# Two blocks of nodes per transpose and per product in three node products of a four-layer graph network

## The reference, cut to what matters

```python
# layer 0: scatter of gated node rows
xp = x @ W_node.T + b_node
msg = gate[:, None] * xp[col]
summed = segment_sum(msg, row)
...
# layer 3: two convolutions
def gcn_conv(x, src, dst, W, b, n_nodes):
    ...
    h = x @ W
    msg = h[src] * norm[:, None]
    out = segment_sum(msg, dst)
    return out + b
h = relu(gcn_conv(x, src, dst, W1, b1, n))
return gcn_conv(h, src, dst, W2, b2, n)
```

## Time and profile before

| | us |
|---|---|
| median of 3 runs | 14080.94 |
| the runs | 14061.56, 14080.94, 14081.86 |
| the profiled execution | 14056.44 |
| its span, first to last instruction | 14053.5 |
| PE busy | 6581.5 (47%) |
| DVE busy | 6540.1 (47%) |
| ACT busy | 1956.0 (14%) |
| POOL busy | 8844.8 (63%) |

### The profile page before, as it was taken

One profiled execution on the slowest core, in us unless ns is written; L12 is line 12 of the kernel. 1 busy time (PEld: TensorE's weight loads), 2 busy tenths in 40 slices (PEclk: granted clock), 3 DMA queues, 4 the chain that ended last, 5 costly groups with the idle time before them and its releaser, 6 DMA issues.

```text
span 14053.5 us, 162350 instructions
## 1 busy us (share of the span) xinstructions
PE 6581.5 (47%) x40047; PEld 5632.1 (40%) x40048; DVE 6540.1 (47%) x13266; ACT 1956.0 (14%) x3268; POOL 8844.8 (63%) x8158
## 2 busy tenths in 40 slices
PE   5777777774555555788500000284333334333334
PEld 4777777774555555677400000173111112111112
DVE  5444444444666666899500000397434344434344
ACT  1111111111222222566300000000000001000000
POOL 2888888884777777100377777402777773777773
PEclk7666666666777777899655555697555555555555
DMA  4333333333444444333122222232111111111111
GB/s 96 18 18 18 18 18 18 18 18 62 126 126 127 126 126 127 107 98 99 50 54 54 54 54 55 61 97 63 39 39 39 39 39 33 39 39 39 39 39 26
DMA packets 851569, 827.49 MB, mean 59 GB/s; under 512 B 630205, under 2 KB 636579, under 8 KB 848948
## 3 DMA queue, kind: packets, MB, share of 16 engines
q0 software_dynamic: 450064, 387.16, 18.7%
q1 hardware_dynamic: 398252, 436.72, 9.9%
q10 hardware_dynamic: 3218, 3.20, 0.1%
HBM read 571.32 MB, written 255.06 MB: 59 GB/s over the span
## 4 chain that ended last, share of the span: by engine, by line
POOL 51%; issue 22%; PE 11%; DMA 8%; DVE 5%; SPq 1%; DVEq 1%; POOLq 0%; ACT 0%; ACTq 0%
POOL tab L728 21%; POOL aux L702 10%; POOL lane_tab L685 10%; DMA lane_tab<-rows,idx 7%; POOL buf_b L702 6%; POOL acc_w L702 4%; PE ps L1089 3%; PE ps L1200 1%; PE ps L979 1%; PE ps L1136 1%; PE ps L1122 1%; DVE buf_b L1658 1%; SPq L552 1%; POOL t_first_tab L713 1%; PE ps L963 1%
## 5 line engine op out<-in xcount | busy, mean ns | idle before, releaser
L728 POOL DMA_INDIRECT tab<-gcn_tab,idx x3136 | 2984.0, 952 | 1826.1 <-issue 1825.2
L685 POOL DMA_INDIRECT lane_tab<-rows,idx x1664 | 2597.7, 1561 | 661.8 <-issue 659.0
L1101 PE MATMUL ps<-ident_b,zero_b 128*128 128x512 bf16 x1664 | 773.2, 619 | 2917.7 <-issue 1551.2
L1737 DVE TENSOR_REDUCE buf_d<-ps 128x512 f32<-128x1536 f32 x416 | 731.1, 1757 | 2299.8 <-PE ps L1105 2299.8
L702 POOL DMA_INDIRECT aux<-att_tab,idx x1568 | 1486.9, 948 | 477.7 <-issue 477.7
L1101 PEld LDWEIGHTS ps<-ident_b,zero_b 128*128 128x128 bf16 x1664 | 182.0, 128 | 3282.1 <-issue 1788.3
L702 POOL DMA_INDIRECT buf_b<-src_tab,idx x832 | 838.3, 1008 | 414.1 <-issue 253.4
L1003 PE MATMUL ps<-ident,srcg 128*128 128x128 f32 x3328 | 695.2, 393 | 727.1 <-DVE srcg L1356 727.1
L702 POOL DMA_INDIRECT acc_w<-src_tab,idx x832 | 815.6, 980 | 253.6 <-issue 247.2
L1003 PEld LDWEIGHTS ps<-ident,srcg 128*128 128x128 f32 x3328 | 643.8, 297 | 772.7 <-DVE srcg L1356 772.5
L1179 PE MATMUL ps<-ident,acc_w 128*128 128x128 f32 x13 | 3.0, 422 | 1954.5 <-ACT idx L819 1954.5
(11 more groups left out here) (297 smaller groups left out, 14373.0 us busy)
## 6 DMA issues: line engine op xcount, KB each, us to landing
y_stash<-buf_c SPq DMA_DIRECT2D x208, 512.0 KB, 2.8
tab<-y_stash SPq DMA_DIRECT2D x208, 512.0 KB, 3.3
aux<-in_edge_attr_dram SPq DMA_DIRECT2D x1696, 32.0 KB
h_stash<-aux SPq DMA_DIRECT2D x196, 264.0 KB, 2.0
tab<-gcn_tab,idx POOLq DMA_INDIRECT x3136
buf_c<-h_stash SPq DMA_DIRECT2D x156, 264.0 KB, 2.7
lane_tab<-rows,idx POOLq DMA_INDIRECT x1664, 3.2
aux<-att_tab,idx POOLq DMA_INDIRECT x1568
```

Source lines behind the costliest of these rows:

```text
L685: pool.indirect_dma_start(lane_tab[k][:, :], bass.IndirectOffsetOnAxis(ap=idx[:, b, u:u + 1], axis=0), rows[:, b, u, 0:D1], None, compute_ ...
L728: pool.indirect_dma_start(g_rows[k][:, u, :], None, table[:, :], bass.IndirectOffsetOnAxis(ap=idx[:, k % RING, u:u + 1], axis=0)).then_inc ...
L1101: pe.matmul(ps[:, 4 * (q % 2) + c, :].rearrange("p (k f) -> p k f", f=P), zero_b[:, :], bc(ident_b[:, :].unsqueeze(1), [P, 4, P]), start=T ...
L1737: dve.tensor_reduce(g_sum[b], parts(4 * b), AX.X, ALU.add).then_inc(s.split_joined, 1)
```

## The change

The products of the first scatter and of both convolutions take two blocks at a time. A pair of blocks, 128 nodes x 128 features, is transposed at once, straight from `x_n` or `tab_d` without ACT's copy to `xs`. The weight stands twice on the diagonal of a 128x128 tile with zeros elsewhere (`twice_n` in the accumulator's space, `twice_g` in `aux`), so one product with 128 rows of contraction gives both blocks' results side by side. DVE makes the tile by a memset and two copies: once before the first product, and at the start of each `gcn`. The second copy of `w1` and `w2` in partitions 64 to 127 comes from two more DMAs. There are 7 steps (PAIRS) of 7 pairs, written out without a loop; DVE takes a step out of PSUM with one instruction. PE waits for ACT's kept source rows before the first product's transposes. The products of layers 1 and 2 keep their code.

```diff
+WPP = 2 * WPC
+PAIRS = W // WPP
+NODE_AT = (0, PAIRS, PAIRS + CHUNKS, PAIRS + 2 * CHUNKS, 2 * PAIRS + 2 * CHUNKS)
...
+        x_pairs = [aux_flat[:, xt_at + k * WPC * P:xt_at + (k + 1) * WPC * P] for k in range(2)]
+        twice_n, twice_g = acc_flat[:, 0:P], aux_flat[:, 2 * S:2 * S + P]
...
-        w12 = sb("w12", [D, 2, D])
+        w12 = sb("w12", [P, 2, D])
...
-            sp.dma_start(w12[:, 0, :], w1).then_inc(s.weights_loaded, 16)
-            sp.dma_start(w12[:, 1, :], w2).then_inc(s.weights_loaded, 16)
+            for at in (0, D):
+                sp.dma_start(w12[at:at + D, 0, :], w1).then_inc(s.weights_loaded, 16)
+                sp.dma_start(w12[at:at + D, 1, :], w2).then_inc(s.weights_loaded, 16)
...
+            def pair_copies(base):
+                for c in range(PAIRS):
+                    act.wait_ge(s.node_xt, c + (base + 1))
+                    act.wait_ge(s.node_products, c + (base + 1))
+                    act.activation(x_pairs[c % 2], ps_flat[:, (c % 2) * 1024:(c % 2) * 1024 + WPC * P], ACT.Copy).then_inc(s.node_xt_copied, 1)
...
-            node_copies(0, x_n)
+            pair_copies(NODE_AT[0])
...
+            def pair_product(base, view, rhs):
+
+                def transposes(c):
+                    at = (c % 2) * 1024
+                    for k in range(WPC):
+                        w = c * WPP + 2 * k
+                        last = pe.transpose(ps_flat[:, at + k * P:at + k * P + P], view[:, w:w + 2, :].rearrange("p w f -> p (w f)"), ident[:, :])
+                    last.then_inc(s.node_xt, 1)
+
+                transposes(0)
+                for c in range(PAIRS):
+                    if c + 1 < PAIRS:
+                        transposes(c + 1)
+                    pe.wait_ge(s.node_xt_copied, c + (base + 1))
+                    pe.wait_ge(s.node_evacuated, c + (base + 1))
+                    at = 2048 + (c % 2) * 1024
+                    for k in range(WPC):
+                        last = pe.matmul(ps_flat[:, at + k * P:at + k * P + P], x_pairs[c % 2][:, k * P:k * P + P], rhs, start=True, stop=True)
+                    last.then_inc(s.node_products, 1)
...
-            node_product(0, wt[0:D, TN:TN + D], D, 4)
+            pe.wait_ge(s.src_kept, 1)
+            pair_product(NODE_AT[0], x_n, twice_n)
...
-            node_product(3 * CHUNKS, w12[:, 0, :], D, 4)
+            pair_product(NODE_AT[3], tab_d, twice_g)
...
+            def twice(to, weight):
+                link(dve.memset(to, 0.0))
+                for at in (0, D):
+                    link(dve.tensor_copy(to[at:at + D, at:at + D], weight[at:at + D, :]))
+
+            twice(twice_n, wt[:, TN:TN + D])
             dve.sem_inc(s.node_in, 1)
...
+            def pairs_out(base, to, bias):
+                for c in range(PAIRS):
+                    dve.wait_ge(s.node_products, c + (base + 3))
+                    at = 2048 + (c % 2) * 1024
+                    dve.tensor_tensor(to[:, c * WPP:(c + 1) * WPP, 0:D], ps_flat[:, at:at + WPP * D].rearrange("p (w f) -> p w f", f=D),
+                                      bc(bias, [P, WPP, D]), ALU.add).then_inc(s.node_evacuated, 1)
+                dve.wait_ge(s.node_evacuated, base + PAIRS + 2)
...
+                twice(twice_g, w12[:, conv, :])
                 dve.memset(acc_w[:, :, :], 0.0).then_inc(order, 1)
```

More of the change, by code:

```diff
@@ L63 @@
 EPS = 1e-5
-assert 0 < AHEAD and LREST == RING and LONG * G * D3 <= 4 * W * D and LONG * G == P and TPOS >= (S + W) * P and 7 * TREG <= 2 * W * D and TREG >= SPAD and TURNS * RING * G == S and SPAD == S + RING * G and SB == TB and CHUNKS * WPC == W and CHUNKS % 2 == 0 and ITER % 2 == 0 and ITER * PAIR == S and CH <= 512 and SROWS * D1 // P % ZEROS == 0
+assert 0 < AHEAD and LREST == RING and LONG * G * D3 <= 4 * W * D and LONG * G == P and TPOS >= (S + W) * P and 7 * TREG <= 2 * W * D and TREG >= SPAD and TURNS * RING * G == S and SPAD == S + RING * G and SB == TB and CHUNKS * WPC == W and PAIRS * WPP == W and CHUNKS % 2 == 0 and ITER % 2 == 0 and ITER * PAIR == S and CH <= 512 and SROWS * D1 // P % ZEROS == 0
 def build(nc, x, src, dst, ea16, ea64, w_edge, b_edge, w_node, b_node,
@@ L710, in _ @@
             for c in range(CHUNKS):
-                pool.wait_ge(s.node_evacuated, 2 * CHUNKS + c + 3)
+                pool.wait_ge(s.node_evacuated, NODE_AT[2] + c + 3)
                 for w in range(c * WPC, (c + 1) * WPC):
@@ L822, in _ @@
             act.wait_ge(s.node_in, 3)
-            node_copies(CHUNKS, x_n)
+            node_copies(NODE_AT[1], x_n)
             indices(s.l1_indices)
@@ L868, in _ @@
             act.wait_ge(s.node_in, 5)
-            node_copies(2 * CHUNKS, x_n)
+            node_copies(NODE_AT[2], x_n)
             act.wait_ge(s.l1_indices, RING * (TURNS + 1))
@@ L896, in _ @@
             act.wait_ge(s.node_in, 6)
-            node_copies(3 * CHUNKS, tab_d)
+            pair_copies(NODE_AT[3])
             split_parts(1)
@@ L904, in _ @@
             act.wait_ge(s.node_in, 7)
-            node_copies(4 * CHUNKS, tab_d)
+            pair_copies(NODE_AT[4])
             std(5)
@@ L921, in _ @@
             last.then_inc(s.tile_rows, 1)
-            pe.wait_ge(s.weights_loaded, 16 * 7)
+            pe.wait_ge(s.weights_loaded, 16 * 9)
             i64 = ident[0:D, 0:D]
@@ L955, in _ @@
             pe.sem_inc(s.node_products, 2)
+            def pair_product(base, view, rhs):
[15 more added lines that the diff above has]
+                    last.then_inc(s.node_products, 1)
             def node_product(base, rhs, n, per_bank):
                 def transposes(c, k):
-                    pe.wait_ge(s.node_xs, c + (base + 1))
+                    pe.wait_ge(s.node_xs, c + (base + (1 - PAIRS)))
                     pe.sem_inc(s.passed, 1)
@@ L1037, in _ @@
             pe.wait_ge(s.node_in, 3)
-            node_product(CHUNKS, wt[0:D, TS:TS + 4 * D], 4 * D, 2)
+            node_product(NODE_AT[1], wt[0:D, TS:TS + 4 * D], 4 * D, 2)
             pe.wait_ge(s.node_in, 4)
@@ L1162, in _ @@
             pe.wait_ge(s.node_in, 5)
-            node_product(2 * CHUNKS, wt[0:D, TA:TA + D2], D2, 4)
+            node_product(NODE_AT[2], wt[0:D, TA:TA + D2], D2, 4)
             def to_rows(n, cols):
@@ L1336, in chunks @@
                 dve.wait_ge(s.node_evacuated, base + CHUNKS + 2)
[L1338 to L1342, removed]
+            def pairs_out(base, to, bias):
[5 more added lines that the diff above has]
+                dve.wait_ge(s.node_evacuated, base + PAIRS + 2)
             dve.sem_inc(s.node_evacuated, 2)
-            chunks(0, to_tab0)
+            pairs_out(NODE_AT[0], tab, bias0[:, :].unsqueeze(1))
             dve.sem_inc(s.node_in, 1)
@@ L1581, in to_att_tab @@
                 last.then_inc(s.node_evacuated, 1)
-            chunks(2 * CHUNKS, to_att_tab)
+            chunks(NODE_AT[2], to_att_tab)
             dve.wait_ge(s.stage_free, 2 * CHUNKS + 2)
@@ L1706, in _ @@
             split(0, lambda to, start, end: dve.tensor_tensor(to, x_n[:, start:end, :], dinv_bc[:, start:end, :], ALU.mult))
[L1708 to L1712, removed]
             def parts(bank):
@@ L1747, in _ @@
             dve.sem_inc(s.node_in, 1)
-            chunks(3 * CHUNKS, lambda c, k: to_acc(c, k, 0))
+            pairs_out(NODE_AT[3], acc, bias3[:, 0:1, :])
             split(1, lambda to, start, end: dve.scalar_tensor_tensor(to, sums_d[:, start:end, :], 0.0, dinv_bc[:, start:end, :], ALU.max, ALU.mult))
@@ L1754, in _ @@
             dve.sem_inc(s.node_in, 1)
-            chunks(4 * CHUNKS, lambda c, k: to_acc(c, k, 1))
+            pairs_out(NODE_AT[4], acc, bias3[:, 1:2, :])
             link(dve.tensor_tensor(sums_d, sums_d, x_n[:, :, :], ALU.add))
```

4 lines of the change are left out of this document (2 added, 2 removed).

## The result

The changed kernel takes 13971.9 us, median of five runs (13913.25 to 13974.2). The kernel before, run beside it, takes 14080.94 (14031.81 to 14119.43). The ratio is 0.9937, with a 95% interval from 0.9908 to 0.9966. The forecast said 13935. The median is inside the range, 37 us above the forecast, and almost on the time of rival (a), though not for rival (a)'s reason. As a gain it is further off: by the ratio 0.63% (0.34 to 0.92), some 89 us of 14080.94, where the forecast had 146 us, 1.04%.

What follows compares the result with a forecast made beforehand. PE's pace in three node products, on the path, was taken as bound. Convolutions 93.6, first product 44.7, small edits -1.2, scatter loop 3.4 sum to 140.5 us saved: 13935 us, between 13915.9 and 13940.4; range 13905 to 13982.

Steps and rivals of the forecast that it cites:

- rival (a): All three changed products stay at 1.2 GHz: 101.4 us saved, about 13970 us; chance 0.12.
- The bound of a step (PE alone): In the three products PE sets the pace, copies and additions fit underneath; 4.81 us per step before, 2.54 at full clock after.
- the equal cost of an instruction of either shape: On PE, a 128x128 f32 product costs what a 64x64 one does, about 0.21 to 0.22 us per instruction at 1.2 GHz.
- the choice of rows 6: Profile rows of 128x128 products in loops, taken to show the new products reach 2.4 GHz about 5 us after PE's start.
- (b): The clock rises in only some of the products, or late: 105 to 130 us saved; chance 0.14 shared with the copy-or-addition rival.
- the base: Time before, from which savings are taken: profiled execution 14056.44 us or median 14080.94, giving 13915.9 or 13940.4; rivals use 14070.
- What bounds the kernel now: Opening step: the three node products lie on the path, bound by PE; convolutions' products run at 1.2 GHz, 67.3 us each.
- Rival (c): ACT's copy or DVE's addition becomes the bound of the new steps: 8 us in all; chance 0.14 shared with (b).
- (d): The gain is hidden by POOL's or a DMA's work beside the products: about 14070 us; chance 0.03.
- (e): Slower: unrolled code makes later loop turns fetch their body, 2.0 us each over 102 turns, 14134 us; chance 0.03.
- Small edits: Making the diagonal weight delays each convolution's first gather by 0.63 us, -1.2 us in all; extra weight loads cost nothing.
- The scatter loop's warm start: The loop after the first product starts at 2.4 GHz; its first two groups of 16 instructions take 2.02 us each, saving 3.4.

Runs made afterwards that it cites:

- Experiment 3: The kernel before, with 26 unused products of the identity put on PE just ahead of layer 1's node product: 14028.8 us, ratio 0.9992.
- experiment 9: The kernel before, unaltered, profiled once more on a chip with slower transfers: 15735.79 us.
- experiment 5: The kernel before, with 128 moving columns (both weights side by side) and still 64 rows in the convolutions' products: 14086.32 us, one run.
- the halves: The changed kernel with each pair's product split in two of 64 columns, 128 rows kept: 13973.81 us, one run.
- experiments 8 to 11: On slower chips: the kernel before with the three products' loops written flat (15701.72, 15709.12 us), the kernel before unaltered (15735.79), the changed kernel unaltered (15591.36).

## Why the prediction came out as it did

**Where it was right.** The bound of a step (PE alone), the equal cost of an instruction of either shape, and the choice of rows 6 against the rule that rival (a) cites. Forecast and measured: a step at full clock 2.54 and 2.32 us; ACT's copy 0.9 to 1.0 and 0.92; DVE's addition 1.07 and 1.09; the clock risen after 5 us (3.2 to 9), and 4 to 8; the first product saved 44.7 and 44.6; a convolution 46.8 and 48.7 or 48.3. The step was put 0.22 us too long: 0.16 of it in the transposes (13902.15 - 13901.39 = 0.76, not 0.92; the wider loaded part costs nothing) and 0.06 in the products (13903.71 - 13902.15 = 1.56, not 1.62). In the first product that was spent again on a start partly at the lower clock (its first 14 transposes took 2.75 us; the granted clock is 0.50 from 182 to 184 us and 1.00 from 184 on), where the forecast had no fall. Two slips in its sums change nothing: 17.8 + 2.5 + 0.33 + 1.1 is 21.73, not 21.8, and (b)'s 105 us less than the base of 14070 is 13965, not 13968.

**The step that failed: "What bounds the kernel now", the clock.** It took the granted clock of one profile as a property of each product: the convolutions always at 1.2 GHz, layer 1's product always at 2.4. Experiment 3 shows a convolution of the old form risen, beside a cold one in the same execution, and experiment 9 shows layer 1's product cold in the unaltered kernel before, as experiment 5 does in a kernel whose code is the same up to there. Two errors follow. First, layer 1's product stood in no term, because the change leaves its code alone; its level is worth 49 us, and the profiled run had it cold; the median of the result is of the group that fits this. The forecast named a stretch outside the three products that moves by more than 10 us as a sign of being wrong, and this is one. The forecast's own sum for the profiled execution, with this product warm as in its base, was 13915.9; the profiled run less 49.1 is 13921.7, and the lower group of runs is 13913 to 13930. Second, the base. The forecast noted that before's runs spread over 25 us "with no order in them". Most of it is these levels: 29 us for each convolution at 46 or 75, some 28 for the first product at 43 or 71, 49 for layer 1's. Before's 38 runs go from 13971 to 14119, that is 148 us, and all four levels together make 29 + 29 + 28 + 49 = 135. The forecast took 140 us from every execution, from a base near 14075 with both convolutions cold. The mean of before's 38 runs is 14054.7 and that of the changed kernel's eleven 13949.4: 105 us between them.

**Rival (a), the clock stays at 1.2 GHz,** gave 13970, which is the time measured, and is wrong in every part: all three products ran at 2.4 GHz after their starts. The Trainium skill ("TensorE: Matmul & The Clock Gate", Part 4, PE-mode transpose) has the full clock not engage for transposes. In the product above a third of PE's instructions are transposes and the granted clock is 1.00 from 13901 to 13913 us, so by this trace the rule doesn't hold for a mixed stream. A time that agrees with a rival is no evidence for it; the stage lengths are.

**Rival (b)** was right in kind for the kernel before and for the halves, not for the pairs. **Rival (c):** the copy takes 0.92 us and has the 1.56 of the products; it didn't come up. **(d)** Nothing was hidden. **(e)** In kind it seems to be there: with flat code a later pass is 3 to 5 us longer (experiments 8 to 11). In size that is 0.1 us per turn at most, in a pass of 50 turns, where the rival needed 1.4.

**Small edits.** The diagonal weight in a convolution was put at -0.6 each, because its cover was thought used up. Timeline of the kernel after at the start of the second convolution, against the earlier trace rows:

```profile
11834.43 0.32 SPq L650 DMA_DIRECT2D gcn_tab<-tab  x1
...
11838.71 5.80 DVE L1759 MEMSET acc_w<- 128x6890 f32 x1 [1.50 <-issue]
...
11844.76 0.94 POOL L734 DMA_INDIRECT tab<-gcn_tab,idx  x1 [132.02 <-issue]
```

The store starts at 11834.43 and takes the same 9.30 us in the chain of waits, so it lands at 11843.73; POOL's first gather starts 1.03 us after that. Before it was 11880.99 - 11879.96 = 1.03 as well. In those 1.03 us POOL works through its own queue, and the clearing (done at 11844.51) ends within them. The cover was 0.96 us (before, the clearing was done at 11880.03), not none: cost 0 instead of -1.2. The scatter loop's warm start was put at +3.4: its first 16 instructions took 3.03 and the next 3.57 us, not 2.02. The granted clock is 0.63 from 200 to 204 us and 0.61 from 204 to 209, after pauses of PE of 2.00 and 1.41 us, and 1.00 from 209 on; that the pauses brought it down is likely, not shown. It gave 0.8 + 0.2 = about 1 us.

## What to carry to other kernels

Before a forecast rests on a stretch at half clock, look whether other stretches of the same shape stand at the other level, compare the spread of the runs with what the levels are worth, and give every dense product its two lengths, the untouched ones as well. Two kernels are then compared over many runs, or with these products warmed in both: five runs of each put the gain at 89 us by the ratio and 109 by the medians, and all runs at 105. Two blocks per product on a diagonal weight pay even at an equal clock (59 us here in three products), because an f32 product costs PE the same for 64x64 as for 128x128 (at 2.4 GHz the 14 instructions of 7 products take 1.77 us in the earlier trace rows and 1.73 in the timeline after). Where an f32 product follows a long idle time of PE, products of the identity issued in that idle time bring it in warm at no cost that shows: in the changed kernel they took away the upper group of times.

## What the runs showed of the hardware

- A dense f32 product that begins after PE has idled 10 to 143 us starts at 1.2 GHz and either rises within 3 to 8 us or stays there to its end: 46.2 or 75.4 us, 54.9 or 104.0, 36.7 or 59.8, with PE equally dense in both. The Trainium skill ("TensorE: Matmul & The Clock Gate", Part 1) has the clock follow how busy PE has been and says that the count of slow products differs from run to run. Here it is not only the count: the product of 104.0 us never rises. What decides between the levels is not shown by these runs. The 128x128 shape rose in each of 8 cases.
- Entered at 2.4 GHz, all warmed products kept it: layer 1's 4 times of 4 and the convolutions' 4 of 4. The first product of single blocks, which begins 2.2 us after PE's transposes before it, mostly doesn't: in six of seven profiles it falls to 1.2 GHz in its first 6 us and stays there (68.4 to 72.0 us), in the seventh it falls and rises again (43.0); with pairs of 128x128 it was at 2.4 GHz throughout in two of five profiles (22.7) and fell for 3 to 4 us near its start, then rose again, in three (23.8).
- At 1.2 GHz the columns of an f32 product between 64 and 128 are nearly free: 75.4 and 76.8 us for the same 196 product instructions.
- Two other chips run this kernel some 11% slower, in stages full of transfers: the second convolution, from its first gather to the scaling of its sums, takes 2318 us in place of 2042, layer 1's loop 3017 in place of 2176. Stages that wait for transfers were compared within a chip only.
